# A vision tower on one core: gray sums and the residual's normalisation one step later, maxima sent from ScalarE's queue, the prologue in another order

## What is computed

```python
gray = einsum('bchw,c->bhw', x, (0.2989, 0.587, 0.114))
edge = sum over two Scharr filters of |conv(gray)| / 2        # one token per image row
h = concat(cls_tok, edge)                                      # [32, 257, 256]
h = h + causal_attention(layernorm(h))                         # 16 heads of 16
xq = fake_quant(layernorm(h))     # one scale: the largest |value| of the whole tensor
y  = silu(xq @ Wg.T) * (xq @ Wu.T)                             # weights fake-quantised by row
h = h + fake_quant(y) @ Wd.T      # again one scale over the whole tensor
```

## Time and profile before

| | us |
|---|---|
| median of 3 runs | 1163.3 |
| lowest and highest | 1157.46, 1168.16 |
| the profiled execution, its time | 1157.32 |
| the profiled execution, its span | 1155.6 |
| TensorE busy in the span | 989.1 |
| VectorE, ScalarE, GpSimd busy | 814.8, 686.6, 538.1 |
| mean granted TensorE clock, of 2.4 GHz | 0.955 |

### The profile page before, as it was taken

The page is one execution under the profiler, slowest core; times in us unless marked ns, Lnnn a source line. Parts: engine busy times, 40 slices in busy tenths (PEclk is TensorE's granted clock), DMA queues, the critical chain, the costliest instruction groups (busy, mean ns, idle before and its releaser), DMA issues. The chain is left out here.

```text
span 1155.6 us, 28368 instructions
## 1 busy us (share of the span) xinstructions
PE 989.1 (86%) x9742; PEld 709.7 (61%) x9742; DVE 814.8 (71%) x1969; ACT 686.6 (59%) x1171; POOL 538.1 (47%) x685
## 2 busy tenths in 40 slices
PE   6768989899999999899999998999888888887665
PEld 5446766666667676667676676676676643333454
DVE  4565566766677777766777777666666449998787
ACT  1345555666666566666666666665553237876776
POOL 5335455565555655565556555655443242220000
PEclk7888999999999999999999999999998989998989
DMA  7665555555556555555565555453422005501874
GB/s 200 149 138 145 132 136 143 133 128 134 133 154 151 137 148 148 129 130 138 152 152 135 149 148 130 130 139 100 116 63 63 12 1 200 200 1 50 265 227 151
DMA packets 156017, 152.93 MB, mean 132 GB/s; under 512 B 28175, under 2 KB 152372, under 8 KB 153908
## 3 DMA queue, kind: packets, MB, share of 16 engines
q1 hardware_dynamic: 154440, 152.14, 48.7%
q10 hardware_dynamic: 1516, 0.01, 0.1%
HBM read 67.49 MB, written 28.35 MB: 83 GB/s over the span
## 5 line engine op out<-in xcount | busy, mean ns | idle before, releaser
L580 ACT ACTIVATE prob<-ST 128x772 f32<-128x772 f32 x256 | 209.5, 818 | 152.4 <-PE ST L1022 147.7
L788 DVE TENSOR_REDUCE mneg<-SX 128x2 f32<-128x258 f32 x256 | 107.5, 420 | 224.7 <-PE SX L1008 224.5
L1005 PE MATMUL SX<-kst,qst 96*128 96x257 bf16 (+1 forms) x1024 | 160.4, 250 | 18.3 <-DMA qst<-qpart 7.6
L790 DVE TENSOR_REDUCE mneg<-SX 128x2 f32<-128x514 f32 x256 | 173.9, 679 | 0.0
L1022 PE MATMUL ST<-qst,kst 98*128 98x256 bf16 (+2 forms) x1536 | 138.0, 222 | 16.3 <-DMA qst<-mpart 15.9
L465 POOL TENSOR_SCALAR_AFFINE_SELECT prob<-prob 128x1016 f32<-128x1016 f32 x128 | 142.6, 1114 | 0.0
L1008 PE MATMUL SX<-mask_s,ident_b 128*128 128x256 bf16 x512 | 142.4, 278 | 0.0
L1022 PEld LDWEIGHTS ST<-qst,kst 98*128 98x128 bf16 x1536 | 120.3, 99 | 34.5 <-DMA qst<-mpart 14.7
L1005 PEld LDWEIGHTS SX<-kst,qst 96*128 96x128 bf16 x1024 | 91.9, 99 | 64.3 <-issue 28.4
L1041 PE MATMUL G<-prob,vaug 128*32 128x256 f32 (+2 forms) x3072 | 116.2, 280 | 11.9 <-POOL prob L465 10.6
L1041 PEld LDWEIGHTS G<-prob,vaug 128*32 128x32 f32 x3072 | 82.7, 111 | 44.6 <-POOL prob L465 16.0
(11 more groups left out here) (232 smaller groups left out, 2056.9 us busy)
## 6 DMA issues: line engine op xcount, KB each, us to landing
kst<-kpart SPq DMA_DIRECT2D x192, 128.5 KB, 2.5
xin<-in_x SPq DMA_DIRECT2D x96, 256.0 KB, 4.1
gst<-gray_dram SPq DMA_DIRECT2D x96, 256.0 KB
qst<-qpart SPq DMA_DIRECT2D x192, 128.0 KB, 2.4
h_dram<-hb SPq DMA_DIRECT2D x8, 1280.0 KB, 4.6
gray_dram<-gray SPq DMA_DIRECT2D x64, 128.0 KB, 3.0
result<-oy SPq DMA_DIRECT2D x32, 256.0 KB, 3.6
hb<-h_dram SPq DMA_DIRECT2D x5, 1280.0 KB, 6.6
```

Of the source, the lines that this page charges most:

```text
L580: nc.scalar.activation(prob[:, g % 2, 2 * (u % 2):2 * (u % 2) + 2, 0:QEND], ST[:, :, 0:QEND], ACT.Exp).then_inc(exp_done, 1)
L788: nc.vector.tensor_reduce(mneg[:, 0, u // 4, 0, at], SX[:, :, S0:S0 + P + 1], AX.X, ALU.max, negate=True)
L790: nc.vector.tensor_reduce(mneg[:, 1, u // 4, 0, at], SX[:, :, S1:S1 + T], AX.X, ALU.max, negate=True).then_inc(max_done, 1)
L1005: mm(SX[:, r, at:at + k], qst[par][0:SR, 2 * u + r, P * t:P * t + P], kst[par][0:SR, 2 * u + r, 0:k], start=t == 1, stop=False)
```

## The change

* SyncE: one DMA loads a whole image (before: three), one saves `gray` (before: two). `max_rows` is gone from it. In step 1 the load of image 2 and of the gate weights stand behind the gathers. `load_down` moves from the end of step 32 into step 33. In step 3 three of the six `qst` DMAs are issued by ScalarE.
* ScalarE: `send_max(0)`, a wait and a DMA, stands behind the copy L638 and ahead of `exponential(bS,0)`; `send_max(1)` at the end of the step behind the gray scaling. The bias loads stand behind step 0.
* GpSimd: the two gray sums stand behind `select(bT,1)` of the next step, and behind them `rstd2` of image `bR = n-7`. The fills of `vaug` and `kst` are split by buffer.
* VectorE: `resid_stats` and the `x2` group now belong to `bR = n-7` and stand behind `maxima(bS,0)` and `maxima(bS,1)`. The pipeline has one more step (`LAST = 7`). The gate weights are quantised in step 2 altogether; the down weights at the front of step 36.
* TensorE: gate and up tiles are turned into `ST` instead of `SX`: four at the end of step 3, and two each behind scores 0, 1, 2 and 3 of step 4, with their copies on ScalarE.
* In the last steps the four `yun` DMAs of image 31 are issued by ScalarE.

The diff, cut to its core:

```diff
-        LAST = 6
+        LAST = 7
...
             def load_x(b, par):
...
-                for c in range(CH):
-                    sp.dma_start(xin[par][:, c, :, :], src[:, c]).then_inc(x_loaded[par], 16)
+                sp.dma_start(xin[par][:, :, :, :].rearrange("p c t w -> p (c t) w"), src).then_inc(x_loaded[par], 16)
...
-            def max_rows(b, par, half_):
-                if valid(b):
-                    wait(sp, msplit, b, 2, half_ + 1)
-                    sp.dma_start(qst[par][SR:SR + 2, 8 * half_:8 * half_ + 8, :], mpart[half_][:, :]
-                                 ).then_inc(m_loaded[half_], 16)
...
-                max_rows(bT, odd, 1)
...
-                    for t in range(QT):
-                        sp.dma_start(gray_dram[odd][1 + P * t:1 + P * t + P, 1:1 + IMG],
-                                     gray[:, t, :]).then_inc(gray_saved, 16)
...
+                    sp.dma_start(gray_dram[odd][1:1 + IMG, 1:1 + IMG].rearrange("(t p) w -> p t w", p=P),
+                                 gray[:, :, :]).then_inc(gray_saved, 16)
...
-                max_rows(bS, par, 0)
...
-                    for s, i in enumerate(Q_SLOT):
+                    for s, i in enumerate(Q_SLOT[:3] if isinstance(n, int) and n == 3 else Q_SLOT):
...
 GpSimd:
                 select(bT, 1)
+                if valid(bW):
+                    wait(pool, gray_scaled, bW, 3, 3)
+                    wait(pool, gray_saved, bC, 16, 16)
+                    src = lambda c: xin[1 - par][:, c, :, :]
+                    nc.gpsimd.tensor_tensor(gray[:, :, :], src(0), src(1), ALU.add).then_inc(gray_step, 1)
+                    wait(pool, gray_step, bW, 2, 1)
+                    nc.gpsimd.tensor_tensor(gray[:, :, :], gray[:, :, :], src(2), ALU.add).then_inc(gray_step, 1)
...
+                if valid(bR):
+                    wait(pool, ln2, bR, LN, LN)
+                    wait(pool, x2_step, bR - 1, XS, XS)
+                    nc.gpsimd.tensor_tensor(rstd2[:, rows2(bR)], ve2[:, :], half[:, :], ALU.pow
+                                            ).then_inc(rs2_done, 1)
...
                 select(bS, 0)
-                if valid(bO):
...
-                if valid(n):
...
 ScalarE:
+                def send_max(half_):
+                    if valid(bS):
+                        wait(act, msplit, bS, 2, half_ + 1)
+                        act.dma_start(qst[par][SR:SR + 2, 8 * half_:8 * half_ + 8, :], mpart[half_][:, :]
+                                      ).then_inc(m_loaded[half_], 16)
...
                     nc.scalar.copy(qpart[:, 1, :, :], qr[:, :, :]).then_inc(q_mid, 1)
+                send_max(0)
                 exponential(bS, 0)
...
                         nc.scalar.mul(xin[par][:, c, :, :], xin[par][:, c, :, :], GRAY[c]).then_inc(gray_scaled, 1)
+                send_max(1)
...
 VectorE:
-            scales(0)
-            quantise(0, range(0, NW0))
...
                     nc.vector.reciprocal(den[:, :], den[:, :]).then_inc(rec_done, 1)
+                if isinstance(n, int) and n == NW2:
+                    scales(2)
+                    quantise(2, range(KC))
...
+                resid_stats(bR)
                 maxima(bS, 1)
+                if valid(bR):
+                    wait(dve, rs2_done, bR, 1, 1)
+                    for t in range(QT):
+                        nc.vector.tensor_scalar(x2[:, t, :], ...)
...
                 maxima(bS, 2)
                 edge_tile(bC, 0)
...
                 maxima(bS, 6)
-                resid_stats(bO)
...
                 maxima(bS, 7)
-                if valid(bO):
-                    wait(dve, rs2_done, bO, 1, 1)
...
 TensorE:
                 if ends and n == 4:
-                    pe.wait_ge(w_copied, 2 * IT)
...
                 scores(0)
+                if ends and n == 4:
+                    turn(range(4, 6))
...
-                if ends and n == 3:
-                    turn(range(0, IT))
...
                 if ends and n == 3:
-                    turn(range(IT, 2 * IT))
+                    turn(range(0, 4))
```

More of the change, by code:

```diff
@@ L159, in vit_tower @@
         qr = sb("qr", [P, KC, IMG])
-        kst = [sb(f"kst{i}", [SR + 2, H, T], bf16) for i in range(2)]
+        kflat = [sb(f"kst{i}", [SR + 2, H * T], bf16) for i in range(2)]
+        kst = [k[:, :].rearrange("p (h t) -> p h t", h=H) for k in kflat]
         qst = [sb(f"qst{i}", [SR + 2, H, IMG], bf16) for i in range(2)]
@@ L621, in step @@
                 exponential(bT, 3)
+                first = isinstance(n, int) and n == 4
+                if first:
+                    place_weights(range(4, 6))
                 absolute(0)
@@ L624, in step @@
                 exponential(bT, 4)
+                if first:
+                    place_weights(range(6, 8))
                 keys(1)
                 exponential(bT, 5)
+                if first:
+                    place_weights(range(8, 10))
                 queries(0)
@@ L629, in step @@
                 exponential(bT, 6)
+                if first:
+                    place_weights(range(10, 12))
                 if valid(bP):
@@ L647, in step @@
                                              scale=rs1[:, t:t + 1]).then_inc(xhat_done, 1)
+                if isinstance(n, int) and n == 3:
+                    act.wait_ge(q_low, 1)
+                    for s, i in enumerate(Q_SLOT):
+                        if s >= 3:
+                            act.dma_start(qst[1 - par][s:SR:NS, :, :], qpart[:, i, :, :]).then_inc(qst_loaded[1 - par], 16)
                 unnormalised(1)
@@ L667, in step @@
                     place_weights(range(2 * IT, len(TW)))
+                if isinstance(n, int) and n == B + 5:
+                    act.wait_ge(den_moved, 64 * B)
+                    for j in range(4):
+                        act.dma_start(yun[32 * j + HD:32 * j + 2 * HD, 0:4:2, :], yun[32 * j:32 * j + HD, 1:4:2, :]
+                                      ).then_inc(y_moved, 16)
             pipeline(act, step)
@@ L1160, in step @@
                 scores(1)
+                if ends and n == 4:
+                    turn(range(6, 8))
                 if ends and n == NW2:
@@ L1167, in step @@
                 scores(2)
+                if ends and n == 4:
+                    turn(range(8, 10))
                 scores_t(bT, odd, 5)
@@ L1172, in step @@
                 scores(3)
+                if ends and n == 4:
+                    turn(range(10, 12))
                 scores_t(bT, odd, 6)
@@ L1181, in step @@
                 scores(5)
+                if ends and n == 4:
+                    pe.wait_ge(w_copied, 2 * IT)
                 scores_t(bS, par, 0)
```

129 lines of the change are left out of this document (58 added, 71 removed).

## The result

The changed kernel takes 1219.9 us (median of 4 runs, 1210.16 to 1221.35) against 1160.4 for the kernel before (median of 4, 1155.04 to 1168.16): ratio 1.049, interval 1.045 to 1.054. The forecast was 1169, with 1147 to 1192 as its range, so the result lies above the range, beyond both slow rivals. The profiled execution has a span of 1219.6 us at a mean clock of 0.937; before it was 1155.6.

The account below looks back on a forecast made before the run. TensorE was taken to bound the kernel, busy 94.34 of 102.8 us in four middle steps. Steady steps +11.7, prologue -4 and end -2 gave +6 us, on the median 1163.3 a forecast of 1169, range 1147 to 1192.

Parts of the forecast that it names:

- both slow rivals: The two slower alternatives to the forecast, Rival 1 at 1183 us and rival 2 at 1200 us.
- Gray sums behind select(bT,1): Steady steps: later sums and rstd2 make x2 meet GpSimd's lock, delaying yn and outputs(bT,2): +0.55 us a step.
- Maxima on ScalarE's queue, first half: Steady steps: this DMA's move makes outputs(bT,3) 0.35 us late, bounds 0 and 1.5 us.
- Landing 2.3 us after issue: Steady steps: the first-half maxima's DMA frees TensorE 2.3 us after issue, bounds 2.0 and 3.5 us.
- rival 2: Steady steps: maxima land 3.5 us after issue, about +1.2 us a step more, 1200 us; chance 0.1.
- Second half at nothing: Steady steps: the second-half maxima's issue fits a hole of ScalarE, cost 0, bounds 0 and 0.3 us.
- Edge matmuls lose their wait: Steady steps: x2 no longer stands before the copy mpart, so it comes earlier: -0.4 us where the wait occurs.
- The prologue: Before the steady steps: earlier scores, gate weights and turned tiles sum to -4 us, bounds -8 and +2.
- First scores at 64 to 67: Start of the kernel: sign of a right forecast, TensorE's first scores at 64 to 67 us instead of 71.26.
- Eight tiles, +2.5 us: Step 4: eight turned weight tiles cost +2.5 us beyond TensorE's holes, between 0 and 4.7.
- The end: Last steps: SyncE's issues in steps 33 to 35 shorten, the w_down move counts 0: -2 us, bounds -4 and +3.
- Rival 1: Steady steps: x2's second half also waits for GpSimd's L480, +1.0 us a step, 1183 us; chance 0.23.

Follow-up runs that it names:

- run 12: Changed kernel, with GpSimd waiting for its own result kr (L485) before tick and the second select: 1172.1 us, ratio 1.012.
- run 1: Changed kernel, with GpSimd waiting right behind rstd2 until VectorE has done x2's two tensor_scalars: 1175.6 us, ratio 1.010.
- run 5: Changed kernel, with GpSimd waiting for x2's two tensor_scalars and both halves of the maxima back on SyncE's queue: 1176.8 us, ratio 1.013.
- run 9: Changed kernel, with the gray sums at their old place and the maxima back on SyncE's queue: 1148.5 us, ratio 0.993.
- run 4: Kernel before, with only the maxima moved to ScalarE's queue: 1207.1 us, ratio 1.038.
- run 2: Changed kernel, with the gray sums alone back at their old place: 1191.0 us, ratio 1.026.
- run 3: Changed kernel, with both halves of the maxima back on SyncE's queue at their old places: 1208.5 us, ratio 1.041.
- run 6: The kernel of run 5, with all twelve gate and up weight tiles turned in step 3: 1175.0 us, ratio 1.013.
- run 10: The kernel of run 9, with all twelve gate and up weight tiles turned in step 3: 1148.1 us, ratio 0.992.
- run 8: Changed kernel, with rstd2 ahead of the two gray sums in GpSimd's queue: 1176.2 us, ratio 1.014.

## Why the prediction was wrong, by its own steps

The runs make a table of two edits in an otherwise changed kernel (us, ratio to before):

| | maxima on SyncE | maxima on ScalarE |
|---|---|---|
| gray sums at the old place | 1148.5 (0.993) | 1191.0 (1.026) |
| gray sums at the new place | 1208.5 (1.041) | 1219.9 (1.049) |

By the ratios the maxima's queue alone costs 39 us and the gray sums' place alone 57, both together 66 and not 96: they partly cover each other. I had given the maxima +0.35 us a step and the sums +0.55, some 9 and 14 us.

*Gray sums behind select(bT,1): the step that failed first.* The chain was right up to rstd2: power at 547.15 in a step from 540.54, 6.6 us in; it is ready 6.76 us in. From there the lock was sized wrongly. I let x2's first tensor_scalar meet `L476` (+0.7) and, as the upper end, its second one instruction more. Measured: the first does meet it (`L481` now), but isn't let in behind it; it stands through the next three instructions as well, +2.6 us, and the second meets nothing. The rows could have warned of it. In the earlier trace rows a gap of 2.28 us lies between `L476` and `L480`, because `L480` waits for ScalarE; I carried that gap over. But the sums and `rstd2` fill it: `vcls` starts 6.7 us into the step instead of 4.0 to 4.7, `kr` at 7.3 to 7.4 where it was mostly at 7.2 to 7.7, so its input is there and the row closes. Run 12 shows that the closed row is the cause of most of the loss: 0.24 us of gap behind `kr`, and some 45 us are back.

*The consequence was looked for at the wrong place.* I followed x2's delay to yn and `outputs(bT,2)`. The nearer reader is scores 3, through maxima 2 in the same bank: its wait is 2.1 us, and `yn` then costs TensorE 0.37 us in that step. Where the lock is taken away the forecast's chain does appear: run 1 has waits for yn of 33 us in 25, 1.3 each. I had netted all of GpSimd's later work to -0.1 us a step; with the lock avoided by GpSimd's wait the sums' place costs up to 0.85 (run 5 against run 9, 26.40 and 25.55).

*Maxima on ScalarE's queue, first half.* "Issue 2.0 us later" was right for this edit alone: 13.98 us into the step before, 15.9 in run 4. In the changed kernel it is 18.8, with the lock's delay in it. "Landing 2.3 us after issue" was right in the changed kernel, 569.42 to 571.68, and 2.0 to 2.5 us in its 20 middle steps:

```profile
569.42 0.62 ACTq L605 DMA_DIRECT2D qst<-mpart  x1
```
```profile
571.68 0.54 PE L1038 MATMUL ST<-qst,kst 98*128 98x256 bf16 x6 [0.56 <-DMA qst<-mpart]
```

The gathers are through there, as I had it: they are issued from 560.75, 8.7 us ahead. In run 4 they are issued from 553.74, only 5.0 us ahead of the maxima at 558.70, and the release takes 2.9 to 3.7 us. The share of busy DMA engines (last number but one) in the 2 us before each issue, first in the changed kernel, then in run 4, is 0.00 and 0.87:

```profile
567.40:569.40 2.00, 2.00 (x18) 1.81 (x17) 1.75 (x6) 1.93 (x4) 1.16 (x1) 1.00 0.00 0
```
```profile
556.70:558.70 2.00, 2.00 (x18) 1.81 (x17) 1.76 (x6) 1.92 (x5) 1.80 (x2) 1.00 0.87 160
```

Without the long lock, but with the sums late (runs 1 and 12), the maxima are issued 6.3 us behind the gathers, the share is 0.35 on the median, and the release takes 2.2 to 2.4 us. So 2.3 us was a fair price for the change as I saw it, and with GpSimd waiting for x2 the maxima's queue costs nothing that shows (run 1 against run 5). For the maxima's move with the sums at their old place (runs 2 and 4, 5.0 us behind the gathers, 2.7 to 3.8 us) it was not: there rival 2 with its 3.5 us was nearer, and my ground against it ("the gathers are through by then") false. The runs line up by the distance to the gathers; none moved the gathers alone.

*Second half at nothing.* Right in the changed kernel. In the old order it isn't (34.7 us of waits of exponential 3 in run 4), so the edits need each other here: x2's move makes `mpart` early enough for ScalarE.

*Edge matmuls lose their wait.* Right, it is gone from the list. Run 2 against run 4, in which x2 stands at the new and the old place and the sums at the old in both, is 13 us better by the ratios, but the merged DMAs and the new prologue are in that too.

*What no term had: the clock.* In the changed kernel scores 3 at 562.74 had waited 2.11 us, and the matmuls straight behind them go at the lower level, 1.2 of 2.4 GHz (the granted clock of the stretch from 562.70 to 565.00 is 0.56 on the mean). A step with a fall lasts 1.3 us longer. Of two like holes, at 562 and at 591, one ends with a fall and one without, so such a hole makes a fall possible and no more. In the 20 middle steps the changed kernel loses 2.45 us each, 49 in all. Its eight steps without a fall last 27.5 us on the mean, its twelve with one 28.8; before it was 25.7, and 27.4 in the one step with a fall. So the holes make 1.76 x 20 = 35 us, and the clock 12 x 1.3 less 1.7, 14 us. A forecast that adds holes only misses more than a quarter of the cost.

*The prologue.* "First scores at 64 to 67": 67.19, just past it. "Eight tiles, +2.5 us": step 4 grew from 24.9 to 30.9. The largest wait in it is not the tiles' but again the maxima's DMA, issued at 83.41 and released only 5.5 us later:

```profile
88.92 0.84 PE L1038 MATMUL ST<-qst,kst 98*128 98x256 bf16 x6 [3.81 <-DMA qst<-mpart]
```

With the maxima on SyncE's queue (run 3) the same wait is 0.8 us and step 4 lasts 27.2. But in runs 2 and 12, with the maxima on ScalarE's queue and this wait at 3.3 to 3.4, step 4 lasts 27.7 as well: the granted clock is 0.81 there, 0.71 in the changed kernel. So the queue's wait alone doesn't make the step long; how much is the wait's and how much the clock's is open. Without the tiles step 4 is 25.7 instead of 27.6 (runs 6 and 5) and 25.9 instead of 27.5 (runs 10 and 9), so the tiles are worth +1.7 to 1.9, less than I took. The prologue's net gain of 4 us was there for the taking: run 10 is 5.5 us ahead of the kernel before at step 6.

*The end.* Forecast -2; from the last `spread_rec` to the last maximum the changed kernel is 1.5 us slower, and run 10 likewise. Not followed further.

*Rivals.* Rival 1 (both locks, +1.0 us a step) had the right mechanism at about half its price (1.8 in steps without a fall). Rival 2 did not come true in the changed kernel: its sign, waits for the maxima over 1.5 us a step, isn't there (0.6 on the median). It is there in runs 2 and 4, with the sums at their old place (1.5 and 1.6). Still the maxima's queue costs 9 us in the changed kernel (run 3) and 39 without the late sums, and neither rival had the clock.

## What to carry to other kernels

Before you push work on GpSimd later, write down which of its waits are real gaps and who on VectorE lives in them: once GpSimd runs late, its inputs are all ready, the gaps close, and a VectorE tensor_scalar or SBUF tensor_tensor can stand until the whole row is through. Where such a row must stay, one wait of GpSimd on its own result (0.24 us here) lets VectorE in. And price a moved DMA by when it is issued and by what else is in flight at that time, not by its queue.

## What the runs showed of the hardware

- A VectorE instruction that is held up beside GpSimd can be passed over. x2's first tensor_scalar, issued beside `L481`, was let in behind none of `L481`, `L485` and `L453` (3.01 us in 26 images). With a gap of 0.24 us behind `L485` it got in there (run 12), and in run 8 one got in at a gap of 0.07 us. In run 8 the second got in without a recorded gap, so a gap is enough and may not be needed. The Trainium skill ("SBUF — State Buffer", section on the two separate sides) says that the pair is held for a whole instruction and the other side blocks; the runs agree with that, and add that the waiting side isn't always next in line.
- An SBUF tensor_tensor can be passed over too: in run 8 the addition of edge tile 0, 0.42 us alone, takes 1.46 us from 402.84 on, through tick and select (`L453`, `L455`).
- In the same stretches tensor_reduce isn't held up: 0.69 us at 401.25 in run 8, with GpSimd's `L485` beside it from 401.66.
- A GpSimd instruction on a single partition holds VectorE up like the others: beside `L474` alone x2's first tensor_scalar takes 0.69 us instead of 0.40, in 29 images of run 2 (spans on GpSimd are rough).
- A DMA issue of ScalarE's queue runs beside its own copy: `ACTq L607` and `ACT L635` both start at 558.70 in run 4 and end at 559.34 and 559.32. So this issue cost ScalarE's arithmetic next to nothing; a wait in front of an issue does cost (exponential 3).
- The same 8 KB rows were released 2.0 to 2.5 us after issue where the DMA engines' busy share in the 2 us before was 0 to 0.66 (changed kernel, runs 1 and 12), 2.7 to 3.8 where it was 0.78 to 0.94 (runs 2 and 4), and 5.5 in step 4 of the changed kernel.
